# Starting the expert stage inside the last batch's attention, with the silu table loaded after the last softmax exponential

## The reference

```python
# L1_ffn_ref, h is the layer norm of x, H = 128, I = 64, E = 8, K = 2
logits = xf @ gate_w.T + lb_bias
scores = jax.nn.sigmoid(logits.astype(jnp.float32))
topw, topi = jax.lax.top_k(scores, K)
topw = topw / (topw.sum(-1, keepdims=True) + 1e-08)
out = jnp.zeros_like(xf)
for e in range(E):
    m = topi == e
    sel = m.any(axis=-1)
    wmean = (topw * m).sum() / jnp.maximum(m.sum(), 1)
    y = silu(xf @ expert_gate_w[e].T) * (xf @ expert_up_w[e].T) @ expert_down_w[e].T
    out = out + jnp.where(sel[:, None], y * wmean, 0)
out = out + (silu(x @ shared_gate_w.T) * (x @ shared_up_w.T)) @ shared_down_w.T
x = x + gb * out
```

## Time and profile before

| | us |
|---|---|
| median of 3 runs | 709.08 |
| lowest, highest | 707.75, 710.56 |
| span of the profiled execution, first to last instruction | 705.9 |
| PE busy | 633.8 (90%) |
| DVE busy | 476.2 (67%) |
| ACT busy | 340.6 (48%) |
| POOL busy | 239.6 (34%) |

### The profile page before, as it was taken

The page is one execution under the profiler, slowest core; times in us unless marked ns, Lnnn a source line. Parts: engine busy times, 40 slices in busy tenths (PEclk is TensorE's granted clock), DMA queues, the critical chain, the costliest instruction groups (busy, mean ns, idle before and its releaser), DMA issues.

```text
span 705.9 us, 11080 instructions
## 1 busy us (share of the span) xinstructions
PE 633.8 (90%) x3839; PEld 487.1 (69%) x3839; DVE 476.2 (67%) x1270; ACT 340.6 (48%) x701; POOL 239.6 (34%) x320
## 2 busy tenths in 40 slices
PE   5799899988779899998899999869889998998996
PEld 4366687877556778775678777746768875676774
DVE  5965589786687557626569886688555527766665
ACT  1133464565535464433455465444555544454553
POOL 3424756462754211004557464484310002000000
PEclk9989999999999999999999999999999999999999
DMA  8200000000000000000000000100000000001011
GB/s 272 61 1 1 2 1 1 1 1 1 1 0 1 3 0 1 1 2 1 1 0 1 2 0 1 37 22 1 0 1 1 1 1 1 1 15 31 15 31 30
DMA packets 12174, 9.65 MB, mean 14 GB/s; under 512 B 1804, under 2 KB 10840, under 8 KB 12120
## 3 DMA queue, kind: packets, MB, share of 16 engines
q1 hardware_dynamic: 12120, 8.95, 4.2%
HBM read 6.84 MB, written 2.10 MB: 13 GB/s over the span
## 4 chain that ended last, share of the span: by engine, by line
PE 62%; DVE 21%; ACT 8%; issue 5%; POOL 3%; DMA 1%; SPq 0%; ACTq 0%; POOLq 0%; DVEq 0%
PE ps L840 13%; PE ps L705 10%; PE ps L818 8%; PE ps L990 4%; PE ps L992 4%; PE ps L991 4%; PE ps L664 4%; PE ps L863 2%; PE ps L864 2%; PE ps L725 2%; ACT xn L1108 2%; PE ps L659 2%; PE ps L879 2%; DVE row_max L1441 2%; POOL rstd L518 2%
## 5 line engine op out<-in xcount | busy, mean ns | idle before, releaser
L1172 ACT ACTIVATE probsT<-ps 128x512 f32<-128x512 f32 (+3 forms) x160 | 85.2, 533 | 158.4 <-PE ps L818 158.4
L840 PE MATMUL ps<-v_sb,probsT 128*128 128x129 f32 (+1 forms) x1124 | 151.4, 279 | 3.7 <-ACT probsT L1174 3.7
L840 PEld LDWEIGHTS ps<-v_sb,probsT 128*128 128x128 f32 (+1 forms) x1124 | 137.6, 191 | 8.8 <-ACT probsT L1174 5.5
L1441 DVE TENSOR_REDUCE row_max<-ps 128x1 f32<-128x512 f32 (+2 forms) x144 | 87.4, 619 | 51.2 <-PE ps L713 26.5
L818 PE MATMUL ps<-ident,probs 128*128 128x128 f32 (+1 forms) x562 | 90.2, 276 | 15.7 <-ACT hT L1100 7.8
L1146 ACT ACTIVATE probs<-ps,neg_max 128x512 f32<-128x512 f32 (+7 forms) x158 | 93.0, 620 | 10.4 <-DVE neg_max L1448 8.2
L818 PEld LDWEIGHTS ps<-ident,probs 128*128 128x128 f32 (+1 forms) x562 | 63.1, 139 | 47.6 <-issue 44.0
L554 POOL TENSOR_TENSOR hq<-ha,hp 128x352 f32<-128x352 f32 x32 | 29.8, 932 | 108.2 <-DVE hp L1491 108.2
L705 PE MATMUL ps<-k_high,q_high 128*128 128x512 f32 (+5 forms) x100 | 42.5, 425 | 6.0 <-ACT probs L1146 6.0
L659 PE MATMUL ps<-unpick,ident_b 128*128 128x512 bf16 x196 | 47.4, 383 | 0.3 <-ACT v_sb L1238 0.3
L517 POOL TENSOR_SCALAR minus_mean<-mv 128x4 f32<-128x4 f32 (+1 forms) x16 | 3.8, 237 | 121.5 <-DVE veps L1309 121.3
(11 more groups left out here) (245 smaller groups left out, 1390.0 us busy)
## 6 DMA issues: line engine op xcount, KB each, us to landing
out<-x_sb SPq DMA_DIRECT2D x8, 256.0 KB, 2.3
x_sb<-in_L_attn_x SPq DMA_DIRECT2D x2, 512.0 KB, 5.2
hT_all<-in_L_wmod SPq DMA_DIRECT2D x2, 384.0 KB
rope_cos<-table_cos SPq DMA_DIRECT2D x1, 768.0 KB, 6.3
rope_sin<-table_sin SPq DMA_DIRECT2D x1, 768.0 KB, 7.8
rope_cos<-table_cos SPq DMA_DIRECT2D x1, 256.0 KB, 3.4
rope_sin<-table_sin SPq DMA_DIRECT2D x1, 256.0 KB, 5.0
moe_raw<-in_L_ffn_expert_gate_w SPq DMA_DIRECT2D x1, 256.0 KB, 2.7
```

The costliest lines, as they stand in the source:

```text
L840: mm = pe.matmul(bank(OUT_AT, 0, V_W), probsT[0:size, n % 4, k * P:(k + 1) * P], v_sb[0:size, j, :], start=(c == 0 and k == 0), stop=(c == ...
L1172: ins = act.activation(probsT[:, n % 4, 0:full], bank(TURN, 0, full), ACT.Copy)
L1441: ins = dve.tensor_reduce(dst, ps[:, start:start + width], AX.X, ALU.max, negate=single)
```

## The change

The weight blocks are turned in slots 26 to 29 of batch 1, four or three at a time through bank 6 (ACT copies the high part, DVE subtracts for the low part). Routing is done in three parts (`ROUTES`): 16 tiles in slots 22 to 28, 8 tiles in slots 30 and 31, and the last 8 between the units 5 and 13 of the stage. The sigmoid becomes an exponential on ACT (`decay`) with an addition and a reciprocal on DVE. The marks keep 8 rows instead of 128. `moe_gate_up(0)` and `(1)` stand inside slot 31. The two batches are one run of 40 units. `moe_gate_up` is up to 15 units ahead of `moe_out` (`LEAD`), and the products wait in 16 buffers. The mean weight is applied when the high and low parts are made, not in the down weights. All `keep_clock` of this place are gone (49 products). Every silu of the stage is the Silu function, and the last of the three exponentials (`decay(2)`) stands between silu(4) and silu(5).

```diff
+ROUTES = [(0, TILES), (TILES, TILES + EIGHT), (TILES + EIGHT, 2 * TILES)]
+DECAY_SLOTS = {TILES + 6: 0, TILES + 12: 1}
+W_SLOTS = {TILES + 10: 0, TILES + 11: 1, TILES + 12: 2, TILES + 13: 3}
+PICKED_SLOT = TILES + 14
+ROUTE_AT, LEAD, MOE_DEPTH, LAST_LEAD = 5, 15, 4, 3
+def outs_after(m):
+    if m < LEAD:
+        return 0
+    return (m - LEAD + 1) * (ALL_UNITS - LAST_LEAD) // (ALL_UNITS - LEAD)
+def parts_after(m):
+    return 0 if m < LEAD else outs_after(m) + 1
...
@@ tensor, in the slots of batch 1
+                        if c == 0 and b == BATCH - 1 and s in W_SLOTS:
+                            turn_moe_weights(W_SLOTS[s])
+                        if c == 0 and b == BATCH - 1 and s == PICKED_SLOT:
+                            turn_unselected(0)
+                        if c == n - 2 and b == BATCH - 1 and s == SLOTS - 1:
+                            moe_gate_up(0)
...
+                    if b == BATCH - 1 and s == SLOTS - 1:
+                        moe_gate_up(1)
                     values(s, n - 1)
...
-                keep_clock(GATE, 11 if b + 1 < BATCH else 18)
-            keep_clock(3, 17)
-            keep_clock(0, 10)
...
+            for m in range(2, ALL_UNITS):
+                moe_gate_up(m)
+                if m == 2:
+                    turn_unselected(1)
+                if m == 3:
+                    turn_group(("norm3", GROUPS - 1))
+                if m == 4:
+                    logits(GROUPS - 1)
+                if m == LEAD - 3:
+                    turn_unselected(2)
+                if m == LEAD - 2:
+                    turn_unselected(3)
+                if m == LEAD - 1:
+                    sum_totals()
+                if m == LEAD:
+                    pe.wait_ge(mean_ready, 1)
+                for n in outs_at(m):
                     moe_out(n)
                     if n % UNITS == 1 and n >= UNITS:
                         turn_y(n // UNITS - 1)
+            for n in range(ALL_UNITS - LAST_LEAD, ALL_UNITS):
+                moe_out(n)
+            turn_y(BATCH * GROUPS - 1)
@@ scalar
-            act.activation(rt[0], logits_sb[:], ACT.Sigmoid).then_inc(sigm_ready, 1)
...
+            for m in range(ALL_UNITS):
+                if m == ROUTE_AT:
+                    decay(len(ROUTES) - 1)
+                for n in parts_at(m):
+                    high_part(n)
+                    if n % UNITS == 1 and n >= UNITS:
                         put_y(n // UNITS - 1)
+                silu(m)
...
+                if m == LEAD - 1:
+                    act.wait_ge(mean_ready, 1)
@@ vector
+            for m in range(ALL_UNITS):
+                if m == 2:
+                    last_normalise()
+                if m == ROUTE_AT:
+                    last_logits()
+                for n in parts_at(m):
+                    low_part(n)
+                if m:
+                    moe_product_of(m)
+                if m == ROUTE_AT:
+                    route_scores(LAST)
...
+                if m == ROUTE_AT + 8:
+                    route_sums(LAST)
+                if m % UNITS == 2 and UNITS < m and m // UNITS + 1 < BATCH * GROUPS:
+                    low_input(m // UNITS + 1)
+                if m == LEAD - 1:
+                    mean_of_experts()
```

More of the change, by code:

```diff
@@ new lines, in moe_out, with turn_y @@
+            def moe_out(n):
+                g, u = divmod(n, UNITS)
+                pe.wait_ge(moe_h_ready, n + 1)
+                if u == 0 and g >= 2:
+                    pe.wait_ge(moe_y_ready, g - 1)
+                high, low = (t[:, n % MOE_DEPTH, :] for t in moe_h_parts)
+                three_passes(bank(GATE + g % 2), DOWN_AT + u * P, high, low, u == 0, u == UNITS - 1).then_inc(moe_down, 1)
+            def turn_y(g):
+                pe.wait_ge(moe_y_ready, g + 1)
+                if g >= 2:
+                    pe.wait_ge(out_ready, g - 1)
+                else:
+                    pe.wait_ge(unselT_ready, 3 + g)
+                for t in range(GROUP):
+                    mm = pe.transpose(bank(TURN + g % 2, t * P, (t + 1) * P), moe_y[:, g % 2, t * P:(t + 1) * P],
+                                      ident[:])
+                mm.then_inc(moe_turned, 1)
@@ L944, in _ @@
-                keep_clock(GATE, 4)
-                if b + 1 < BATCH:
+                    keep_clock(GATE, 11)
+                    turn_group(("norm3", GROUPS - 1))
+                    keep_clock(GATE, 4)
                     pe.wait_ge(v_ready, (b + 1) * 2 * GROUPS + 1)
[L947 to L954, removed]
@@ L967, in _ @@
[L967 to L1007, removed]
-                                          ident[:])
-                    mm.then_inc(moe_turned, 1)
-                N = UNITS * GROUPS
-                LEAD = MOE_DEPTH - 1
-                for n in range(LEAD):
-                    moe_gate_up(n)
-                pe.wait_ge(mean_ready, 1)
-                for n in range(N):
-                    if n + LEAD < N:
-                        moe_gate_up(n + LEAD)
@@ L1274, in _ @@
+            for n in range(parts_after(ALL_UNITS - 1), ALL_UNITS):
+                high_part(n)
+            put_y(BATCH * GROUPS - 1)
         @block.vector
@@ new lines, in _, with routing, over_experts, candidates @@
+            LAST = len(ROUTES) - 1
+            def routing(r):
+                start, end = ROUTES[r]
+                n = end - start
+                parts = [t[:, 0:n, :] for t in (key, first, second, rest, weight)]
+                return n, logits_sb[:, start:end, :], parts, [rc[:, k, 0:n] for k in range(8)]
+            def over_experts(t, n):
+                return t.unsqueeze(2).to_broadcast([P, n, EXPERTS])
+            def candidates(r, values, top):
+                n, _, (t_key, *_), _ = routing(r)
+                link(dve.tensor_reduce(top, values, AX.X, ALU.max))
+                link(dve.tensor_tensor(t_key, values, over_experts(top, n), ALU.is_ge))
+                link(dve.tensor_tensor(t_key, t_key, priority[:].unsqueeze(1).to_broadcast([P, n, EXPERTS]), ALU.mult))
@@ L1556, in _ @@
                         combine(s - FFN_LAG)
+                    if b == BATCH - 1 and s in W_SLOTS:
+                        moe_weights_low(W_SLOTS[s])
                     if b + 1 < BATCH and s in (NEXT_SLOT, NEXT_SLOT + 1):
@@ L1688 @@
+            for n in range(parts_after(ALL_UNITS - 1), ALL_UNITS):
+                low_part(n)
+                if n % UNITS == 3:
+                    add_y(n // UNITS - 1)
+            add_y(BATCH * GROUPS - 1)
 _INS = ["L0_attn_x", "L0_attn_Wq", "L0_attn_Wk", "L0_attn_Wv", "L0_ffn_w_gate", "L0_ffn_w_up", "L0_ffn_w_down",
```

428 lines of the change are left out of this document (271 added, 157 removed).

## The result

The changed kernel takes 700.78 us (median of 4 runs, 699.96 to 702.83) where the kernel before takes 709.44 beside it (707.75 to 710.56). The ratio is 0.9885, with a 95% interval from 0.986 to 0.991: 8.7 us less, where 13.9 were forecast. The time lies in the range of the forecast (691 to 702) and 5.6 above the 695.2 that it named.

What follows compares the result with a forecast made beforehand. The stage was taken as bound by PE, behind a serial 25.8 us chain. The new span was 579.8 + 6.3 + 90.6 + 3.0 + 7.4 + 4.9 = 692.0, plus 3.2 to the median: 695.2 us, range 691 to 702.

Steps and rivals of the forecast that it cites:

- Attention +6.3: Attention grows 6.3 us: weight blocks 1.6, marks 0.5, units 0 and 1 3.0, ACT's copies 1.2; routing on DVE nothing.
- PE's work in the stage, 90.6 + 3.0: Behind attention: 379 passes at 0.231 and seven turns, 90.6 us; last turn, logits, 24 mark turns and sums add 3.0.
- Waits 7.4: PE's waits in the joined stage, from product buffers, table loads, routing, mean and clock: 7.4 us, replacing 4.8 before.
- the normalising and DVE's routing: Delays of products on DVE: normalising the last group 0.4 us at unit 2, last routing's 26 small steps 1.1.
- the ring: Pair of PE banks in gate-ups: 3.20 us through silu and product against PE's 3.24 per two units, so no slack.
- The clock's 1.7: Behind the 2.2 us idle at the mean, the clock falls to half speed, costing 1.7 us; ends 0 and 1.7.
- The tail 4.9: From the last down product to the end: 4.9 us, unchanged.
- A: Each ACT table switch costs 1.4 us beyond its load: 698.9 us in all; chance 0.08.
- B: Inserts aren't hidden: ACT's 3.2 all show (+2.0), routing goes over (+3), tables show whole (+1.5): 701.8 us; chance 0.15.
- C: Fewer waits: small steps and ACT's copies hidden, clock holds: 691.2 us, or 692 with one in part; chance 0.10.
- D: Slower than before: products in units 2 to 14 wait 2.1 to 2.9 us more per turn; 709 (chance 0.04), 714 (0.03).
- 11.7 to 12.0 us for five units: Sign to look for in the profile after: time of five units and their down products in the steady part.

## Why the forecast held, and the step that failed

- **Attention +6.3: right.** The values of the last slot end at 586.15, forecast 586.1. The parts fit too: weight blocks and marks, up to the end of slot 30, add 3.1 (forecast 3.3; less the turns that leaves 1.0 for ACT's copies), and slot 31 adds 3.15 (forecast 3.0), with the 0.28 for unit 1's marks in it. silu(0) starts at 584.41, ahead of that, and the load before it at 583.11.
- **PE's work in the stage, 90.6 + 3.0: this is the step that failed.** It took each of the 379 passes at the 0.231 of before, and costed the marks' 8 rows at nothing. The row count of the operands was in the changed code, and the trace of before had the price: its passes with 1 row cost 0.39 the pair and its passes with 96 rows nothing, as shown above. The prediction read neither. It costs 0.28 in each of 31 gate-ups, 8.7 us. "TensorE: Matmul & The Clock Gate" of the Trainium skill, section "Why this matters for your kernels", says that one pass over 32 rows takes as long as one over 128. The listed durations agree (0.38 to 0.39 for 8, 32, 64 and 128 rows), but their ends are modelled; the starts add a price ahead of the pass and behind it. The small extras were a little short: three marks turns take 0.54 each and 0.10 ahead of and behind each, 2.2 where 1.35 stood; sums 0.59 and 0.09 behind them for 0.4. Together 4.2 for 3.0.
- **Waits 7.4: some 4 came.** Here too starts tell more than idles, since a listed duration of 0.40 covers 0.17 of waiting. By starts the tables cost 597.93 - 596.84 - 0.23 = 0.86 and 0.10 more in the next start (1.25 forecast), the mean 619.00 - 616.46 - 0.23 = 2.31 (2.2), the last parts 0.4 (0.3). What is left is 0.25 at 605.41, behind unit 10, and 0.10 in the start after it: the wait for a unit u = 0 (0.4 forecast for it), since DVE was idle for 0.51 ahead of that product. Of the normalising and DVE's routing (1.5 together) nothing shows, and the clock stayed (1.7). The miss above hides them: a gate-up of 1.90 instead of 1.62 gives the ring the slack that the forecast denied it. Added up the stretch is 90.6 + 4.2 + 8.7 + 4.0 = 107.5.
- **With 128 rows** it is 100.1, which leaves 100.1 - 90.6 - 4.2 = 5.3 for waits. The forecast without the clock's 1.7 had 5.7: tables 1.25 (1.27 measured), mean 2.2 (2.3), and 1.7 for the rest against 2.2. So the ring without slack was seen rightly.
- **The clock's 1.7: a chance, put down as a fact.** Behind the same 2.14 to 2.15 it fell in one profile of six, at a price of 1.5.
- **The tail 4.9: right** (693.6 to 698.5). That the clock of before was 1.00 "but for one place" was misread: in the tail it is 0.78, and 0.84 after, with four turns of PE there, so nothing hangs on it.
- **Rivals.** A is excluded by ACT's rows and by the runs without the loads. B named nearly the right time (701.8) for a wrong reason: routing was hidden, ACT's copies cost 1.0 and not 3.2, the tables 1.0 and not 2.8. Of C two parts came, the small steps hidden and the clock held, the first by what made the rest slower; ACT's copies weren't hidden. D didn't occur. That the time lies in the range is luck in part: the range reached up to 702 for B, not for this cost, and the 3.4 of waits that stayed away covered a third of it.
- **A marker that was badly chosen:** "11.7 to 12.0 us for five units". The down products run at 1.48 per gate-up, so a group's turn comes each 9.84 us (661.00 to 690.53 are three groups), and each 9.1 with 128 rows.

In sum: the profile is 579.8 + 6.35 + 107.5 + 4.9 = 698.5, and forecast was 579.8 + 6.3 + 101.0 + 4.9 = 692.0. The 6.5 between are 8.7 for the rows and 1.2 for the extras, less 3.4 of waits that these hid or that didn't come.

The best kernel found is the changed one with marks of 128 rows, 694.4 (ratio 0.9795), or with the mean first besides, 693.2; POOL's clearing of the other 120 rows lies in attention and shows no cost (from the first turn of weight blocks to the last values' end it is 50.8 without it, and 50.8 with it in the variants of 32 and 64 rows).

## What to carry to other kernels

An operand cut to the rows that carry data saved nothing on PE here, and from 64 rows down it cost on both sides of the pass; look at its neighbours, and fill it up with zeros where they have 128 rows. For each edit costed at nothing, look for that shape in the trace, in other stages too: here 36 passes of attention had the price. Where no row shows it, the term needs two ends like the others. And read starts, not durations: from 619.00 to 690.90 PE was busy for all of 71.90 us while it lost 0.28 in each gate-up.

## What was not expected of the hardware

- A bf16 pass with 8, 32 or 64 rows between f32 passes with 128 adds 0.28 us against the same pass with 128 rows: the load behind it starts 0.31 after its own instead of 0.01. A pair of f32 passes with 1 row adds 0.39, and passes with 96 rows add nothing. Why a load beside the running product is then missing wasn't settled: the trace calls the idle "issue". The turns of marks, whose weights have 128 rows but 8 columns, also start 0.10 late and make the second start behind them 0.11 late; no run parts that from their waits.
- The clock falls or stays behind nearly the same idle. Behind 2.14 to 2.15 us it fell in 1 of 6 profiles, each of another variant of the changed kernel. Behind 2.06 and 2.07 it fell in 1 of 2, and there the programs are the same up to that place. One profile can't settle such a term.
- A switch of ACT's table costs its 1.28 us and no more: each of the three stands 0.00 to 0.02 behind the instruction before it.
